# A fused four-layer kernel: the first layer's gates in three bfloat16 parts

## The reference

```
logits = normalize(n) @ normalize(sim) - sigmoid(gates)        # n: layer norm, 256 x 128
masked = where(mask > 0, relu(logits), -inf)                   # at least two experts stay
rw     = softmax(masked)                                       # 256 tokens x 8 experts
q      = einsum('btc,ech,bte->bth', n1, q_proj, rw)            # k, v and o likewise
moe    = einsum('btei,eic,bte->btc', gelu(n2 @ w1), w2, rw2)
```

## Time and profile before

| | |
|---|---|
| median of 3 runs | 1230.87 us |
| the runs | 1229.96, 1230.87, 1235.17 us |
| profiled execution, its span | 1232.8 us (no other time of it is given) |
| TensorE busy | 1077.4 us, 87% |
| VectorE busy | 762.0 us, 62% |
| ScalarE busy | 517.4 us, 42% |
| GpSimd busy | 156.5 us, 13% |

### The profile page before, as it was taken

The page is one execution under the profiler, slowest core; times in us unless marked ns, Lnnn a source line. Parts: engine busy times, 40 slices in busy tenths (PEclk is TensorE's granted clock), DMA queues, the critical chain, the costliest instruction groups (busy, mean ns, idle before and its releaser), DMA issues.

```text
span 1232.8 us, 18221 instructions
## 1 busy us (share of the span) xinstructions
PE 1077.4 (87%) x6758; PEld 768.1 (62%) x6758; DVE 762.0 (62%) x1821; ACT 517.4 (42%) x836; POOL 156.5 (13%) x165
## 2 busy tenths in 40 slices
PE   1799999998658999999999983878999999998855
PEld 0688888887546566667666643645667667666432
DVE  3365556554573677887787775455485675676532
ACT  1235444545321453564476322124645546453410
POOL 0121111100206300000000003012022012021000
PEclk9999999999767999999999985889999999999986
DMA  9000000000200221011300003000000000000000
GB/s 327 21 1 14 14 14 14 14 14 1 101 4 0 74 99 52 1 52 52 119 2 1 1 1 104 1 1 1 1 1 6 6 1 5 6 1 6 6 5 4
DMA packets 13096, 35.25 MB, mean 29 GB/s; under 512 B 3738, under 2 KB 7498, under 8 KB 12240
## 3 DMA queue, kind: packets, MB, share of 16 engines
q1 hardware_dynamic: 12624, 32.61, 7.6%
q10 hardware_dynamic: 288, 1.44, 0.3%
q0 software_dynamic: 96, 0.04, 0.0%
HBM read 33.02 MB, written 1.06 MB: 28 GB/s over the span
## 4 chain that ended last, share of the span: by engine, by line
PE 67%; issue 17%; DVE 9%; ACT 3%; DVEq 2%; POOL 1%; POOLq 1%; ACTq 0%
PE ps L1096 5%; PE ps L1084 5%; PE ps L818 5%; PE ps L1026 5%; PE ps L1001 4%; PE ps L981 3%; PE ps L974 3%; PE ps L1236 3%; PE ps L966 3%; PE ps L1157 3%; PE ps L1137 2%; PE ps L864 2%; PE ps L852 2%; PE ps L1175 2%; PE ps L828 2%
## 5 line engine op out<-in xcount | busy, mean ns | idle before, releaser
L1893 DVE TENSOR_REDUCE arena<-ps 128x8 f32<-128x2048 f32 x32 | 73.3, 2291 | 37.4 <-PE ps L1137 37.4
L1441 ACT ACTIVATE arena<-ps 128x2048 f32<-128x2048 f32 x32 | 60.1, 1877 | 57.4 <-PE ps L1161 57.4
L1084 PE MATMUL ps<-uR,arena 128*128 128x256 f32 x256 | 74.8, 387 | 0.0
L1001 PE MATMUL ps<-arena,uR 128*128 128x512 f32 x128 | 70.3, 631 | 3.1 <-ACT arena L1387 2.9
L1236 PE MATMUL ps<-arena 128*128 128x512 f32 x128 | 68.2, 657 | 5.5 <-DVE xacc L1967 4.5
L1026 PE MATMUL ps<-arena 128*128 128x128 f32 x512 | 69.0, 291 | 3.9 <-DVE arena L1807 3.2
L1096 PE MATMUL ps<-arena 128*128 128x256 f32 x256 | 65.6, 403 | 6.7 <-DVE arena L1874 3.7
L1026 PEld LDWEIGHTS ps<-arena 128*128 128x128 f32 x512 | 64.7, 203 | 8.9 <-issue 7.1
L1414 ACT ACTIVATE arena<-ps 128x512 f32<-128x512 f32 x64 | 37.9, 597 | 61.4 <-PE ps L1085 55.6
L1096 PEld LDWEIGHTS ps<-arena 128*128 128x128 f32 x256 | 49.0, 199 | 20.6 <-issue 9.6
L1791 DVE TENSOR_REDUCE arena<-ps 128x16 f32<-128x512 f32 x64 | 44.2, 691 | 26.2 <-PE ps L1002 22.0
(11 more groups left out here) (376 smaller groups left out, 2380.4 us busy)
## 6 DMA issues: line engine op xcount, KB each, us to landing
arena<-in_skills SPq DMA_DIRECT2D x16, 768.0 KB, 5.6
arena<-in_expert_w SPq DMA_DIRECT2D x2, 2048.0 KB, 8.3
arena<-in_l_experts SPq DMA_DIRECT2D x8, 386.5 KB, 3.1
arena<-in_consts_b ACTq DMA_DIRECT2D x1, 1408.0 KB, 8.2
x2R<-in_x SPq DMA_DIRECT2D x8, 128.0 KB, 2.6
arena<-in_L_w SPq DMA_DIRECT2D x2, 512.0 KB, 8.1
arena<-in_phiC SPq DMA_DIRECT2D x1, 1024.0 KB, 9.0
arena<-in_expert_b SPq DMA_DIRECT2D x1, 1024.0 KB, 5.1
```

Source lines behind the costliest of these rows:

```text
L1001: mm(high[:, c, :], uR[:, b, k * P:(k + 1) * P], phiC[:, col:col + 512], start=True, stop=False)
L1084: mm(o, phiC[:, st_ * P:(st_ + 1) * P], uR[:, b, :], start=True, stop=False)
L1441: av(pexp[:, t, gp].rearrange("p c h t -> p (c h t)"), scores[:, :, :].rearrange("p c t -> p (c t)"), ACT.Exp, scale=SCALE3).then_inc(s.sc ...
L1893: V.tensor_reduce(nm[:, k, :, 2 * gp:2 * gp + 2], scores[:, :, :].rearrange("p c (h t) -> p c h t", h=2), X, ALU.max, negate=True).then_in ...
```

## The change

The 8 gates of a token, float32, are split into three bfloat16 parts whose sum is the gate: the gate rounded to bfloat16, the rest rounded to bfloat16, and what is then left. The parts stand one below the other in the contracted dimension (rows 0 to 7, 8 to 15 and 16 to 23 of each block of 32, rows that were zero), and `selR` has ones in all three places, so that the matmul adds them up. So `gate4`, the transposes, their PSUM view, `gateR` and `selR` become bfloat16; `selR` moves from the float32 block of constants to the other. The order lists and all waits stay as they are.

```diff
+    put("selR", (k[:, None] % 32 < 3 * E) & (k[:, None] % E == 2 * (k[:, None] // 32) + np.arange(2 * P)[None] // P))
-NF32 = CONSTS["selM"][0]
+NF32 = CONSTS["selR"][0]
...
+        gate4 = [[bsw[:, 4 * g + 2 * u, :].bitcast(BF16).rearrange("p (k c r) -> p k c r", k=K, c=4) for u in range(U)]
-        gateR = [ta([P, T]) for _ in range(2)]
+        gateR = [ta([P, T], BF16) for _ in range(2)]
...
+                            last = tr(bank[:, T:T + P].bitcast(BF16)[:, k * P:(k + 1) * P],
+                                      gate4[g][u][:, k].rearrange("p c r -> p (c r)"), identb[:, :])
...
-                        av(gateR[g], bank[:, T:2 * T], ACT.Copy).then_inc(s.gateT_ready, 1)
+                        av(gateR[g], bank[:, T:T + P].bitcast(BF16), ACT.Copy).then_inc(s.gateT_ready, 1)
...
                         V.reciprocal(den1, den1)
                         dr()
                         four = [P, K, 4, E]
-                        V.tensor_tensor(gate4[g][u][:, :, :, 0:E], D.unsqueeze(2).to_broadcast(four),
-                                        den1.unsqueeze(2).unsqueeze(3).to_broadcast(four), ALU.mult).then_inc(s.gate_ready, 1)
+                        V.tensor_tensor(D, D, den1.unsqueeze(2).to_broadcast([P, K, E]), ALU.mult)
+                        dr()
+                        V.tensor_copy(parts[:, :, :, 0:E], D.unsqueeze(2).to_broadcast(four))
+                        dr()
+                        V.tensor_tensor(D, D, parts[:, :, 0, 0:E], ALU.subtract)
+                        dr()
+                        V.tensor_copy(parts[:, :, :, E:2 * E], D.unsqueeze(2).to_broadcast(four))
+                        dr()
+                        V.tensor_tensor(parts[:, :, :, 2 * E:3 * E], D.unsqueeze(2).to_broadcast(four),
+                                        parts[:, :, :, E:2 * E], ALU.subtract).then_inc(s.gate_ready, 1)
```

More of the change, by code:

```diff
@@ L91, in _constants @@
     put("headg", (k[:, None] % 32 // DH == np.arange(4)[None]))
-    put("selR", (k[:, None] % 32 == 2 * (k[:, None] // 32) + np.arange(2 * P)[None] // P))
     c8 = np.arange(8 * P)[None]
+    put("selR", (k[:, None] % 32 < 3 * E) & (k[:, None] % E == 2 * (k[:, None] // 32) + np.arange(2 * P)[None] // P))
     put("selM", (k[:, None] % 32 == 16 * (c8 // (4 * P)) + 4 * (c8 % (4 * P) // P) + c8 % P // 32))
@@ L518, in build @@
         gate_words = bsw.rearrange("p b o -> p (b o)")
-        gate4 = [[bsw[:, 4 * g + 2 * u:4 * g + 2 * u + 2, :].rearrange("p k (c r) -> p k c r", c=4) for u in range(U)]
+        gate4 = [[bsw[:, 4 * g + 2 * u, :].bitcast(BF16).rearrange("p (k c r) -> p k c r", k=K, c=4) for u in range(U)]
                  for g in range(2)]
-        gateR = [ta([P, T]) for _ in range(2)]
+        gateR = [ta([P, T], BF16) for _ in range(2)]
         selR = con("selR").rearrange("k (h p) -> k h p", h=2)
@@ L795, in step_a @@
                         for k in range(K):
-                            last = tr(bank[:, T + k * P:T + (k + 1) * P], gate4[g][u][:, k].rearrange("p c r -> p (c r)"), ident)
+                            last = tr(bank[:, T:T + P].bitcast(BF16)[:, k * P:(k + 1) * P],
+                                      gate4[g][u][:, k].rearrange("p c r -> p (c r)"), identb[:, :])
                         last.then_inc(s.gate_T, 1)
@@ L1620, in step_a @@
                     if n == f"GE{g}":
-                        D, S, den1 = gd[g][u], gs_[g][u], glow[g][u]
+                        D, S, den1, parts = gd[g][u], gs_[g][u], glow[g][u], gate4[g][u]
                         dr()
```

## The result

| | median us | kernel before, same chip | ratio, 95% interval |
|---|---|---|---|
| changed kernel, 4 runs | 1239.64 | 1230.61 (4 runs) | 1.0062 [1.0037, 1.0087] |
| the same again, 11 runs | 1238.32 | 1232.70 (34 runs) | 1.0050 [1.0036, 1.0065] |

The change costs 0.5 to 0.6%, that is 6 to 8 us. The forecast of 1235.2 had the sign, and both medians lie in its range (1225 to 1240), but above the 1232 to 1237 that the forecast gave itself. Its +4.3 us is 2 to 3 us short, and lies just under the lower ends of the two intervals (+4.4 and +4.6 us).

The account below looks back on a forecast made before the run. The prediction took TensorE's full queue to bound the first stage, with VectorE's last gate step on the path at six of sixteen gates. Its terms, -5.5 + 6.2 + 3.6 = +4.3 us, gave 1235.2 us, range 1225 to 1240.

Parts of the forecast that it names:

- Spread: TensorE's eight gate-spreading matmuls (line 807): 0.22 us in bfloat16 instead of 1.07, 0.86 less; 15.2 us over sixteen.
- What is kept of it: Spread gains that survive to the next TensorE stall: 5.5 us at five spreads; the other eleven, 9.7 us, lost.
- my walk: TensorE's shift carried gate by gate through the first stage: 5.5 us kept, 6.2 and 3.6 paid, +4.3 in all.
- The split: VectorE's last gate instruction (line 1633) becomes five with four drains: +1.03 us per gate, 16.5 us over sixteen.
- Six paid gates: Gates whose transposes TensorE already waits for, each later by the added VectorE work: 6 x 1.03 = 6.2 us.
- 1.8 us behind other gates: VectorE steps delayed behind gates GE1.0 and GE0.2 (1.3 us) and GE0.4 (0.5 us), without the memset's share.
- PX: GpSimd copy and memset over gate GE1.0: memset holds the first cast, gate 2.7 us late, 1.8 us more paid.
- Rival 2: At gate GE1.0 the GpSimd memset doesn't hold VectorE's cast: +2.5 us, 1233.4 us; chance 0.22.
- The clock: TensorE falling to half clock in thin first-stage stretches: no cost in the forecast's sum, 1.24 us per fall in a rival.
- Rival 3: Two or three more TensorE clock falls at 87-93, 120-125, 213-231 us: +6.8 or +8.0 us, up to 1238.9; chance 0.19.
- no more than one fall between 50 and 305 us: Sign for the forecast: at most one TensorE clock fall in that stretch; more would point to Rival 3.
- Rivals 1 and 4: First: VectorE absorbs the added work, 1221.9 us, chance 0.11. Fourth: bfloat16 spreads as long as now, 1240.7 us, chance 0.05.

Follow-up runs that it names:

- e_fill: Changed kernel with the eight matmuls of one spread (SPR1.0) issued six times over, in front of a TensorE stall; 1235.25 us, ratio 1.0021.
- e_gain_px: Changed kernel with only the first bfloat16 part (one VectorE instruction per gate) and GpSimd's step PX behind the last gate transposes; 1223.05 us, ratio 0.9931.
- e_before_px: Kernel before with only GpSimd's step PX (copy and memset) moved behind the last gate transposes; 1230.40 us, ratio 0.9993.
- e_cost_px: Kernel before plus the split's four VectorE instructions per gate, written to unused columns, with PX behind the last gate transposes; 1238.31 us, ratio 1.0055.
- e_px: Changed kernel with GpSimd's step PX (copy and memset) moved behind the last gate transposes; 1231.39 us, ratio 1.0003.
- e_gain: Changed kernel with only the first bfloat16 part, one VectorE instruction per gate, the other two parts zero; 1224.66 us, ratio 0.9940.
- e_cost: Kernel before, float32 spread and transposes kept, plus the split's four VectorE instructions per gate, written to unused columns; 1241.38 us, ratio 1.0083.
- e_two: Changed kernel with two bfloat16 parts instead of three, the second by a fused multiply and subtract per half; 1224.21 us, ratio 0.9951.

## Why the prediction was right in sign and short in size

- **Spread: right in kind, mis-sized.** 0.33 us per spread, not 0.22, so the saving is 0.75 us, not 0.86. The four-matmul row gives the pace and not the start: in e_fill 48 matmuls take 1.55 us, which is 0.33 for the first eight and 0.24 for each eight more.
- **What is kept of it: mis-sized, too low.** 5.5 us by my walk, 7.3 by e_gain_px against e_before_px (1223.05 and 1230.40); in their profiles, which have one half-clock stretch each, the last group of the first stage starts 9.4 us earlier (315.63 against 325.04). SPR1.0, SPR1.2, SPR1.3 and SPR1.5, which I had put down as lost, each put TensorE ahead by 0.65 to 0.80 us more by the next spread (SPR1.3 starts at 182.20 and 177.37, SPR0.5 at 194.00 and 188.42).
- **The split: right.** 1.04 us per gate against 1.03. Six paid gates and 1.8 us behind other gates made 8.0 without PX; e_cost_px is 7.9 above e_before_px, which agrees more closely than the runs can tell (in the profiles the first stage's last group starts 6.0 us later, 331.07 against 325.04). Waits of the transposes for VectorE rose from 7.3 to 17.7 us, more than the 6 us I named, since gates with slack came to be waited for as well (nine, not five).
- **PX: right in mechanism, the step that failed in size.** "If the memset holds it, GE1.0 ends near 87.85": it ended at 87.53, behind a cast of 1.87 us, and its multiply had begun 0.33 us earlier than before, so the gate is 2.7 us later against its own start, as forecast; with the memset moved the same cast takes 0.20 us. Rival 2 is refuted. But I priced it at 1.8 us, and the whole collision is worth 6 to 7 in this kernel, as e_px shows (the same move gives about 1 in e_before_px); the memset alone 4.2. The Trainium skill, page "SBUF — State Buffer", section "Who interferes with whom", goes further than the part I used: a VectorE instruction with two SBUF inputs contends with a GpSimd instruction that reads SBUF, and not with one that only writes it, while a cast may contend with both. The rows agree in all three cases: multiply under the copy 1.77 and 1.83 us, cast under the memset 1.87, fused pair beside the memset 0.41. Which of cast and memset asked first, the part of the rule that the prediction used, the rows don't tell: the cast starts at 84.84 us and the memset at 84.86, and the cast is the one that stood still.
- **The clock: what I left out of the sum.** Rival 3 named the place (87 to 93 us) and the form, and I gave it 0.19. Two new stretches came in the first profile of after, at 92 and 105 us, and again, the first of them longer and with a third at 284, in the second. They made 24 instructions 4.49 us instead of 2.94 and eight 3.57 instead of 1.97, 3.15 us together where I had 2 x 1.24; e_px has neither. So rival 3's signs came together with the forecast's own steps, and its 1237.7 to 1238.9 is near where the time lies (by the ratios 1237.0 to 1238.5 on the median that the forecast started from). My "no more than one fall between 50 and 305 us" is the sign that decided it. What brings the falls is not shown: e_gain has both without the split, e_cost has two without short spreads, e_two has the stall and none there.
- **Rivals 1 and 4** fell with e_cost (+10.2) and with the 0.33 us.

With the measured terms the sum is -7.3 + 7.9 + 6 to 7 = +6.6 to +7.6, near what was measured (+5.6 to +9.0). This proves little, since the 6 to 7 is itself the changed kernel less e_px; what it tests is that gain and cost without PX leave +0.6, and e_px stands 1.2 us above e_before_px. That the forecast came as near as 2 to 3 us is in part luck: too small a kept gain and too small a collision have opposite signs.

What stays open: why the collision costs the changed kernel more than the cost alone (6 to 7 against 3.4 us), if it does, since the intervals leave room for both to be equal; what makes the clock fall where it does, since a TensorE with less to do is not enough (7.72 us busy of 10 in the stretch from 88 to 98 in the changed kernel, 9.67 before, but 7.89 in e_two, at full clock throughout); and what moves the 901 to 907 us behind the first stage.

## What to carry to other kernels

When work moves from the full engine to one that the full engine waits for, count the waits at each hand-over, not the busy time: here 12.8 us of busy time off TensorE bought about 7, and 12.8 us more on VectorE cost about 8. Before adding casts or two-input steps to VectorE, look for GpSimd instructions that lie over them, and try moving these first, which gave 6 to 7 us here. Look at the clock behind every new stall: in the changed kernel it took 3.15 us more behind one of 1.87 us, and in e_two, behind one of 1.81, nothing. Then ask for the cheapest form of the split that is exact enough: two parts with a fused second step kept the gain and paid 0.4 us a gate in place of 1.03.

## What the runs showed of the hardware that was not expected

- The cast that began at 84.84 us by the record, 0.02 us ahead of the memset's 84.86, was the one that stood still, for all of the memset's 1.80 us. A recorded start of two engines so close together doesn't tell which was served first.
- Eight packed 32x256 bfloat16 matmuls take 0.33 us of the queue, where four took 0.11 and each eight more in one row took 0.24 (e_fill).
- The same kernel ran MH0.0 at half clock in one execution (3.18 us) and at full clock in another (1.89): one profile does not tell which clock falls belong to a kernel.
- Forty more matmuls in front of a stall made a kernel 3 us faster (1235.25 against 1238.32 us).
- A stall of 1.81 us was followed by full clock (e_two), one of 1.87 by half clock (the changed kernel).
